# A selective-scan layer on four engines: the state's carry and two broadcasts move from VectorE to ScalarE

## What is computed

```python
u, gate = jnp.split(hidden_states @ W_in.T, 2, axis=-1)        # 1024 channels each
u = silu(causal_conv4(u) + conv_b)
dt, Bm, Cm = jnp.split(u @ Wx.T, [32, 48], axis=-1)            # 32 + 16 + 16, each RMS-normalised
delta = softplus(dt @ Wdt.T + dt_bias)
state = exp(delta * A) * state + (delta * u) * Bm              # per channel and per one of 16 states, over t
y = sum_n(state * Cm) + u * D_param
out = (y * silu(gate)) @ W_out.T
```

## Time and profile before

| what | us |
|---|---|
| median of 3 runs | 2125.49 (2113.07 to 2134.3) |
| the profiled execution | 2125.84 |
| its span, first to last instruction | 2124.0 |
| busy in the span: PE, DVE, ACT, POOL | 1695.8, 1449.0, 1089.6, 1042.7 |
| mean granted clock of PE | 0.804 of full |

### The profile page before, as it was taken

One profiled execution on the slowest core, in us unless ns is written; L12 is line 12 of the kernel. 1 busy time (PEld: TensorE's weight loads), 2 busy tenths in 40 slices (PEclk: granted clock), 3 DMA queues, 4 the chain that ended last, 5 costly groups with the idle time before them and its releaser, 6 DMA issues. The chain is left out here.

```text
span 2124.0 us, 24389 instructions
## 1 busy us (share of the span) xinstructions
PE 1695.8 (80%) x8224; PEld 899.6 (42%) x8224; DVE 1449.0 (68%) x2432; ACT 1089.6 (51%) x1988; POOL 1042.7 (49%) x585
## 2 busy tenths in 40 slices
PE   6873999999689975888596887968869687544678
PEld 2510232322265434665273654736547355222332
DVE  3363788887173121079989999899998999988131
ACT  2340666667621112556666566665666756643064
POOL 0000000000053023078998988989889898998102
PEclk8855899999965986887596986969869698556799
DMA  5332000000193446233544435444354443532301
GB/s 207 141 60 39 2 3 3 2 3 3 35 346 113 133 145 227 50 80 80 114 95 96 110 79 107 108 95 110 75 109 110 95 99 83 117 91 62 117 20 60
DMA packets 151262, 192.38 MB, mean 91 GB/s; under 512 B 18245, under 2 KB 123461, under 8 KB 149344
## 3 DMA queue, kind: packets, MB, share of 16 engines
q1 hardware_dynamic: 143250, 168.00, 31.7%
q0 software_dynamic: 4576, 16.79, 2.2%
q10 hardware_dynamic: 3312, 6.03, 0.7%
HBM read 142.60 MB, written 48.18 MB: 90 GB/s over the span
## 5 line engine op out<-in xcount | busy, mean ns | idle before, releaser
L1745 DVE TENSOR_TENSOR_SCAN ssm_scan<-ssm_psum,ssm_state,ssm_scan 128x256 f32<-128x256 f32 x1024 | 683.5, 729 | 26.2 <-ACT ssm_psum L1614 25.9
L1324 POOL TENSOR_TENSOR ssm_scan<-ssm_scan,ssm_bc 128x1024 f32<-128x1024 f32 x256 | 599.8, 2355 | 110.1 <-DVE ssm_state L1748 109.7
L1614 ACT ACTIVATE ssm_psum<-ssm_rep,ssm_a 128x256 f32<-128x256 f32 x1024 | 435.0, 467 | 263.5 <-DVE ssm_scan L1745 262.9
L1448 PE MATMUL ssm_psum<-ssm_scan,ssm_select 128*32 128x256 f32 x2048 | 211.3, 493 | 237.7 <-POOL ssm_scan L1324 232.6
L659 DVE TENSOR_REDUCE att_rowmax<-att_psum 128x1 f32<-128x512 f32 x448 | 278.5, 683 | 73.9 <-PE att_psum L554 73.9
L632 ACT ACTIVATE att_probs<-att_psum 128x1024 f32<-128x1024 f32 x256 | 248.6, 1021 | 151.8 <-PE att_psum L572 151.6
L1309 POOL TENSOR_TENSOR ssm_scan<-ssm_rep,ssm_bc 128x1024 f32<-128x1024 f32 x128 | 301.2, 2354 | 26.8 <-PE ssm_psum L1448 16.6
L1448 PEld LDWEIGHTS ssm_psum<-ssm_scan,ssm_select 128*32 128x32 f32 x2048 | 45.8, 121 | 360.1 <-POOL ssm_scan L1324 263.3
L554 PE MATMUL att_psum<-att_k,att_q 72*128 72x512 bf16 x448 | 161.3, 401 | 35.0 <-DMA att_k<-parts 34.0
L532 POOL COPY att_v<-v_tokens 128x128 f32<-128x128 f32 x8 | 2.3, 292 | 364.6 <-ACT att_out L626 364.6
L1730 DVE TENSOR_TENSOR ssm_scan<-ssm_rep,ssm_psum 128x1024 f32<-128x1024 f32 x128 | 155.5, 1215 | 6.2 <-PE ssm_psum L1448 3.0
(11 more groups left out here) (231 smaller groups left out, 2068.4 us busy)
## 6 DMA issues: line engine op xcount, KB each, us to landing
ssm_rep<-drive_rows SPq DMA_DIRECT2D x256, 256.0 KB, 4.8
qkv_wmod<-in_wmod SPq DMA_DIRECT2D x8, 1536.0 KB, 12.1
moe_we<-in_we SPq DMA_DIRECT2D x8, 1024.0 KB, 14.4
ssm_bc<-bc_rows SPq DMA_DIRECT2D x32, 256.0 KB, 5.2
drive_rows<-ssm_delta SPq DMA_DIRECT2D x64, 128.0 KB, 1.7
drive_rows<-ssm_du SPq DMA_DIRECT2D x64, 128.0 KB, 1.8
sorted_rows<-moe_zeros SPq DMA_DIRECT2D x1, 5888.0 KB, 19.1
moe_sorted<-sorted_rows SPq DMA_DIRECT2D x23, 256.0 KB, 3.4
```

The source lines that it names most:

```text
L1324: nc.gpsimd.tensor_tensor(scan[:, Q % RING], scan[:, Q % RING], bc[:, c % 2, 1, gr, :].unsqueeze(1).to_broadcast([P, J, SW]), ALU.mult).th ...
L1448: last = nc.tensor.matmul(ps_y[t % 2][32 * j:32 * j + 32, :], select[:], scan[:, Q % RING, j, :], start=(gr == 0), stop=False)
L1614: nc.scalar.activation(ps_decay[n % HALF_BANKS][:, i], rep[:, s % 2, 0, j, :], ACT.Exp, scale=amat[:, t, gr, j:j + 1]).then_inc(decay_done, 1)
L1745: nc.vector.tensor_tensor_scan(scan[:, Q % RING, j, :], ps_decay[(2 * Q + j // 2) % HALF_BANKS][:, j % 2], scan[:, Q % RING, j, :], state[ ...
```

## The change

The carry moves from DVE to ACT: `carry(Q - 2)` stands at the head of unit Q's decays, behind the wait for unit Q-2's scans and behind whatever ACT does at position q. The two last ones follow the loop. The C product stays in place and waits for the carry as before. The three broadcast copies go from DVE into three exponentials of ACT that read the logarithm broadcast. Softplus works in place in PSUM: both Relu, then both Abs, then Exp and Ln, with one wait more; the tile `soft` goes. Some places move: the last output projection of a chunk, ("out", 3), from 29 to 28, `CENTRED` from 10 to 11, `RESIDUAL` by one unit for three of its four.

```diff
+    CARRY_LAG = 2
-              24: ("step", 2), 25: ("step", 3), 27: ("out", 2), 29: ("out", 3)}
+              24: ("step", 2), 25: ("step", 3), 27: ("out", 2), 28: ("out", 3)}
-        CENTRED, RMS_WIDE, NORMED, NORM = 10, 18, 21, 22
+        CENTRED, NORMED, NORM = 11, 21, 22
-        RESIDUAL = {18: 0, 19: 1, 29: 2, 31: 3}
+        RESIDUAL = {19: 0, 20: 1, 30: 2, 31: 3}
@@ inverse_rms (ACT)
-                nc.scalar.activation(flat, flat, ACT.Exp, scale=-0.5).then_inc(rms_done, 1)
+                if c >= 1:
+                    act.wait_ge(rb_done, c)
+                for s, (at, n) in enumerate(((0, RANK), (RANK, NST), (RANK + NST, NST))):
+                    nc.scalar.activation(rwide[:, :, at:at + n], rms[:, :, s:s + 1].to_broadcast([P, ST, n]), ACT.Exp, scale=-0.5).then_inc(rwide_done, 1)
@@ step_out (ACT)
-                if n >= 1:
-                    act.wait_ge(soft_done, n)
                 for i in range(2):
                     t = 2 * pair + i
-                    nc.scalar.activation(soft[:, i, :], z[:, i], ACT.Abs, bias=dtb[:, t:t + 1]).then_inc(abs_done, 1)
                     nc.scalar.activation(delta[:, t, :], z[:, i], ACT.Relu, bias=dtb[:, t:t + 1]).then_inc(relu_done, 1)
+                act.wait_ge(relu_done, 2 * n + 2)
+                for i in range(2):
+                    t = 2 * pair + i
+                    nc.scalar.activation(z[:, i], z[:, i], ACT.Abs, bias=dtb[:, t:t + 1]).then_inc(abs_done, 1)
                 act.wait_ge(abs_done, 2 * n + 2)
-                nc.scalar.activation(soft[:], soft[:], ACT.Exp, scale=-1.0).then_inc(expneg_done, 1)
+                nc.scalar.activation(z, z, ACT.Exp, scale=-1.0).then_inc(expneg_done, 1)
                 act.wait_ge(expneg_done, n + 1)
-                act.wait_ge(relu_done, 2 * n + 2)
-                nc.scalar.activation(z, soft[:], ACT.Ln, bias=1.0).then_inc(soft_done, 1)
+                nc.scalar.activation(z, z, ACT.Ln, bias=1.0).then_inc(soft_done, 1)
+            def carry(Q):
+                t, gr = Q % UNITS // GROUPS, Q % GROUPS
+                act.wait_ge(scan_done, (Q + 1) * J)
+                nc.scalar.copy(state[:, t, gr, :], scan[:, Q % RING, :, SW - 1]).then_inc(carry_done, 1)
@@ decays (ACT)
                     if n >= HALF_BANKS:
                         act.wait_ge(scan_done, 2 * (n - HALF_BANKS + 1))
+                    if half == 0 and Q >= CARRY_LAG:
+                        carry(Q - CARRY_LAG)
@@ unit (DVE)
-                dve.wait_ge(scan_done, (Q + 1) * J)
-                nc.vector.tensor_reduce(state[:, t, gr, :], scan[:, Q % RING, :, SW - 1:SW], AX.X, ALU.max).then_inc(carry_done, 1)
```

More of the change, by code:

```diff
@@ L1130, in state_space @@
         bc = sb("ssm_bc", [P, 2, 2, GROUPS, SW])
-        soft = sb("ssm_soft", [P, 2, SW])
         delta = sb("ssm_delta", [P, DT, SW])
@@ L1145, in state_space @@
          norm_done, h_done, halo_in, halo_saved, proj_done, upre_out, conv_done, conv_out, u_done, wx_done, proj_out, stat_done, rlog_done,
-         rms_done, rwide_done, rb_done, normed_done, bc_stored, b_set, wdt_done, abs_done, expneg_done, soft_done, relu_done,
+         rwide_done, rb_done, normed_done, bc_stored, b_set, wdt_done, abs_done, expneg_done, soft_done, relu_done,
          delta_done, du_done, drive_stored, decay_done, dve_input, pool_input, scan_done, carry_done, read_done, sum_done, summed,
@@ L1150, in state_space @@
              "norm_done h_done halo_in halo_saved proj_done upre_out conv_done conv_out u_done wx_done proj_out stat_done rlog_done "
-             "rms_done rwide_done rb_done normed_done bc_stored b_set wdt_done abs_done expneg_done soft_done relu_done "
+             "rwide_done rb_done normed_done bc_stored b_set wdt_done abs_done expneg_done soft_done relu_done "
              "delta_done du_done drive_stored decay_done dve_input pool_input scan_done carry_done read_done sum_done summed "
@@ L1672, in _ @@
                     decays(c, q)
+            for Q in range(SCH * UNITS - CARRY_LAG, SCH * UNITS):
+                carry(Q)
         @block.vector
@@ L1701, in save_halo @@
                                         ).then_inc(halo_saved, 1)
[L1703 to L1708, removed]
             def rms_norm(c):
@@ L1773, in _ @@
                 save_halo(0, pair)
-            rms_wide(0)
             rms_norm(0)
@@ L1789, in _ @@
                             save_halo(c + 1, SAVE_HALO[q])
-                        if q == RMS_WIDE:
-                            rms_wide(c + 1)
                         if q == NORMED:
```

## The result

The changed kernel takes 2187.9 us (median of 4 runs, 2183.2 to 2192.2), the kernel before 2119.3 in the runs beside it: a ratio of 1.031, 95% interval 1.024 to 1.038. The forecast was slower, 2178, in a range of 2112 to 2213. The kernel before had been put at 2125.8 in the forecast, so 52 us of loss were expected and 69 came. The profiled execution took 2184.07 us, its span 2182.3.

The account below looks back on a forecast made before the run. PE was taken to bound each chunk's first half, with DVE, POOL and ACT tight in the second. 2125.8 + 44 (all chunks) + 7.5 (clock) = 2177.5, said as 2178 us, range 2112 to 2213.

Parts of the forecast that it names:

- What bounds the kernel: PE bounds units 0 to 18 of a chunk; DVE, POOL and ACT are tight in the second half.
- ACT's instructions: On ACT: a carry issues in 0.11 us, P starts 0.25 after its start, a softplus step lasts 2.9.
- The first half: PE idles 2.95, 0.6, 1.8 and 2.0 us more at units 2, 8, 11, 15; net at sum(18) +5.1.
- rival (c): Idles at units 11 and 15 also drop the clock, 28 us on top of all of unit 2: 2213; chance 0.15.
- The second half: Behind modulation and softplus steps, P(23) comes +2.5 us later and P(25) +0.6; out 2 and 3 give -1.0.
- the roundings: Remaining roundings in the sum for one chunk, +0.2 us.
- the clock: PE's idle at unit 2 could cost 2.1 us a chunk, 15 in seven; half was taken, 7.5.
- The sum: One chunk +7.4 us; all eight chunks together +44; with 7.5 for the clock, 2177.5, say 2178.
- (a): POOL's backlog hides the carries' delay and DVE's saved time comes through: faster, 2068; chance 0.17.
- (b): Gains and delays cancel if carry(1) and carry(15) meet a late PE: +12, 2138; chance 0.13 together with (d).
- (d): Carries are moved but DVE waits elsewhere for the same time: no change, 2126; chance 0.13 together with (b).
- the signs: P(1) 6.2 us after projection 0, period 140 to 143, POOL's carry wait over 150, DVE busy 60 to 75 less.

Follow-up runs that it names:

- carry_first: The changed kernel with each carry still on ACT, but ahead of ACT's other work at its position: 2095 us, ratio 0.988 to the kernel before.
- early_3_4: The changed kernel with the carry ahead of ACT's other work at positions 3 and 4 only: 2169 us, ratio 1.025 to the kernel before.
- early_steps: The changed kernel with the carry ahead of ACT's other work at positions 24, 25, 27 and 28 only: 2147 us, ratio 1.015.

## Why the prediction was right, point by point

**What bounds the kernel.** Right: the two halves of a chunk and PE's hold on the first. The places where PE would idle came within 0.1 us: 3.72, 0.64, 1.78 and 1.97 us for a forecast of 3.7, 0.6, 1.8 and 2.0. That they are caused by the order and not by the size is shown by carry_first.

**ACT's instructions.** A carry takes 0.09 us of issue (forecast 0.11), P starts 0.27 us behind it (forecast 0.25), a softplus step lasts 2.79 us (forecast 2.9). Exp and Ln in PSUM take 0.58 us each, against 0.63 and 0.60.

**The first half.** Sum(18) comes 7.9 us late, forecast 5.1. The walk was made at full clock. Unit 2 paid 0.44 in the sum and 1.16 in the convolution, and unit 15, which I had put into rival (c), paid 0.83 in the sum and skip and 0.85 in out 0: together 3.3 us in this chunk. Of the 3.26 us of idle before sum(18) nothing stayed, where I had left 0.8.

**The second half.** P(23) comes 20.5 us after sum(18) instead of 16.8: +3.7, forecast +2.5. P(25) follows 9.76 us later (forecast 9.8). From out 2 (1454.30) to the next projection 0 (1473.82) it is 19.5 us, before 21.4: -1.9 where I had -0.8 with the roundings. Of this, 0.9 is the clock: out 2 took 5.05 us where it had taken 5.96. PE is at half clock from sum(19) to 23; it was at half clock before as well (0.50 in the earlier trace rows), so my full-clock durations for the rms, skip and broadcast products there were too short. DVE waits 1.18 us for the broadcast product there. This explains the 1.2 in direction; no run isolates it.

**The sum.** The stage grew by 66.2 us, where the forecast had 44 and 7.5 for the clock. Chunk by chunk (distances between the copies of B): chunk 0 grew by 3.7 us (forecast 5), chunks 1 to 5 by 11.8 and then 10.3 each (forecast 7.4 and 1.05 for the clock), chunk 6 by 13.9 (forecast 7), and the last one lost 4.3 (forecast 5). Two terms were mis-sized. The clock was taken at half of 15 us; at units 2 and 15 it cost 3.3 us in each of six chunks and 1.7 once more at unit 11 of chunk 6, 21 us in all. Some of that came back at out 2 and sum(18), 1.3 us in a middle chunk. And chunk 6 was put at 8 us with its share of the clock, and took 13.9; of the difference 3.9 is the clock, and the rest is open. Two small slips of the sum changed nothing: 3.26 less 0.8 at unit 18 is 2.5 and not 2.6, and the three terms add up to 2177.3 and not 2177.5.

By the rule of the Trainium skill, page "TensorE: Matmul & The Clock Gate", section "What's actually happening", that an idle array falls back to the lower clock, I had written 2185; 2188 was measured. The trace agrees with it at units 2 and 15, where the matmuls behind 3.72 and 1.97 us of idle were slower. That the number came so close is luck. I had charged unit 2 alone, with 2.1 us, and it paid 1.6; unit 15, not charged, paid the rest; and the forecast started from 2125.8 us, 6.5 above the median of the kernel before.

**What the parts give.** The exponentials off DVE were worth 24.5 us in the stage and not 18. The places were worth 22 in the stage but 11 by medians, for 12 expected, so it isn't shown that they were mis-sized; nor which of the three gives how much, since they were run together. The carry costs 112 us in the stage (111 by medians), where the forecast of 52 for the whole, with 18 and 12 for the others, leaves 82 for it. So it was luck that the errors went against each other: the exponentials, and perhaps the places, took back part of what the carry cost too much.

**The rivals.** (a), that POOL's backlog covers the delay, fell: at units 11 and 23 POOL stood idle until ACT's carry, 4.42 and 2.14 us, and P(1) followed 0.28 us behind it. (b) and (d) fell with the ratio. (c) happened in part: unit 15 lost clock in every chunk from 1 to 6, unit 11 only in chunk 6. Of the signs, DVE's busy time fell by 61 us (60 to 75 forecast) and POOL's wait for the carries grew to 174.0 us (beyond 150), while the period of 143.4 us lies a little above the 140 to 143.

## What to carry to other kernels

When a small step of a chain moves to another engine, look at what stands before it in that engine's list, not at its own duration: 0.2 us of copy delayed a product by 4 us, since it stood behind work that itself waits for the end of the chain. Putting the small step first at its own place in the list does not help if the work of the place before is what delays it, as P(23) shows. A gain on one engine (here 61 us of DVE's busy time) can be had only where that engine bounds; here PE bounds one half of every chunk, and POOL's own work, 116 us a chunk, is near in the other. Parts of a change should be timed apart: two of this one were worth 2.4% together (interval 1.7 to 3.0%), and the third hid them.

## What the runs showed of the hardware that was not expected

PE's idle before sum(11) had the same length in every middle chunk of the change and of early_3_4, 1.78 or 1.79 us, and did not have the same result. In the change the gate product behind it took 3.62 us, except in chunk 6, where it took 5.30. In early_3_4 it took 5.17 to 5.20 us in chunks 1, 3 and 5, and 3.62 in chunks 2, 4 and 6. One might think that it matters whether PE has already fallen to half clock at unit 2 and risen again, as it does in the change. The trace of early_3_4 speaks against that: the convolution behind sum(2) took 3.72 us, at full clock, in all six.

Other places show the same. Behind 1.97 us of idle (the change, before sum(15)) the eight small matmuls took 0.95 us, and behind 2.51 us 0.64, as at full clock. And once the clock fell with no idle just before: the rms product behind sum(18) of the change (1415.91) took 1.00 us where it takes 0.65 in early_steps. What PE did just before it there was 16 matmuls of one column and the sum. So the price of an idle could not be read from its length alone; what decides it stays open.
